# The softmax inverse of the middle stage moves from VectorE to GpSimd

## The reference

```
y = _cond_layer_norm(x, cond, ...)
scores = (q[src] . k[dst]);  ex = exp(scores - smax[src])
attn = ex / denom[src];      out = segment_sum(attn * v[dst]) @ wo + bo
x = x + out
y = relu(_cond_layer_norm(x, ...) @ m_w1 + m_b1) @ m_w2 + m_b2
x = x + y
```

## Time and profile before

| | |
|---|---|
| median of 3 runs | 1299.51 us (1297.67 to 1301.1) |
| the profiled execution | 1292.61 us, span 1290.8 us |
| mean granted TensorE clock | 0.955 |
| TensorE busy | 1171.9 us, 91% of the span |
| TensorE weight loads busy | 1058.0 us, 82% |
| VectorE busy | 831.9 us, 64% |
| GpSimd busy | 656.0 us, 51% |
| ScalarE busy | 487.3 us, 38% |
| the four bodies of the middle stage | about 290 to 815 us of the span |

### The profile page before, as it was taken

One profiled execution on the slowest core, in us unless ns is written; L12 is line 12 of the kernel. 1 busy time (PEld: TensorE's weight loads), 2 busy tenths in 40 slices (PEclk: granted clock), 3 DMA queues, 4 the chain that ended last, 5 costly groups with the idle time before them and its releaser, 6 DMA issues. The chain is left out here.

```text
span 1290.8 us, 21357 instructions
## 1 busy us (share of the span) xinstructions
PE 1171.9 (91%) x7134; PEld 1058.0 (82%) x7134; DVE 831.9 (64%) x1759; ACT 487.3 (38%) x873; POOL 656.0 (51%) x807
## 2 busy tenths in 40 slices
PE   7888779689999999999999999899999899999686
PEld 6778667569988998889988998778888688888674
DVE  7999787666766567566667576355556555565545
ACT  5334424124612353225521452344344343443311
POOL 3443562356557555766477555844116332235562
PEclk9889889689999999999999999999999989999788
DMA  5000001311212120230112113240010000011101
GB/s 112 1 1 1 22 10 59 117 47 40 74 42 74 52 75 1 75 91 10 66 42 74 43 65 121 73 122 1 1 66 34 1 33 1 1 66 33 65 33 40
DMA packets 40265, 60.81 MB, mean 47 GB/s; under 512 B 13864, under 2 KB 14114, under 8 KB 39537
## 3 DMA queue, kind: packets, MB, share of 16 engines
q1 hardware_dynamic: 40162, 59.47, 14.3%
HBM read 52.76 MB, written 5.41 MB: 45 GB/s over the span
## 5 line engine op out<-in xcount | busy, mean ns | idle before, releaser
L405 POOL TENSOR_SCALAR prob<-prob,rinv 125x628 f32<-125x628 f32 x160 | 126.2, 790 | 290.5 <-DVE rinv L399 289.1
L335 POOL TENSOR_TENSOR w_lo<-w_raw,w_hi 128x512 fp32r<-128x512 f32 x152 | 203.5, 1339 | 12.7
L295 PE MATMUL ps<-yt_hi,w_hi 128*128 128x314 f32 x640 | 203.1, 317 | 5.1 <-DVE yt_lo L1898 3.0
L295 PE MATMUL ps<-yt_hi,w_lo 128*128 128x314 f32 x640 | 198.5, 310 | 0.0
L295 PE MATMUL ps<-yt_lo,w_hi 128*128 128x314 f32 x640 | 198.2, 310 | 0.0
L633 PE MATMUL ps<-oh_s,oh_d 125*125 125x314 bf16 x800 | 124.4, 315 | 23.4 <-DVE oh_s L531 20.9
L633 PEld LDWEIGHTS ps<-oh_s,oh_d 125*125 125x125 bf16 x800 | 111.0, 145 | 36.6 <-DVE oh_s L531 30.3
L295 PEld LDWEIGHTS ps<-yt_hi,w_hi 128*128 128x128 f32 x640 | 122.6, 192 | 7.7 <-DVE yt_lo L1898 3.6
L358 ACT ACTIVATE pt_hi<-ps 125x625 fp32r<-125x625 f32 x160 | 108.1, 685 | 51.3 <-PE ps L317 50.6
L317 PE MATMUL ps<-ident,prob 125*125 125x125 f32 x800 | 117.7, 282 | 8.9 <-DVE pt_lo L1709 5.7
L332 POOL TENSOR_SCALAR w_hi<-w_raw 128x512 fp32r<-128x512 f32 x152 | 98.0, 645 | 53.9 <-DMA w_raw<-L_gnn_wo 37.4
(11 more groups left out here) (263 smaller groups left out, 2736.8 us busy)
## 6 DMA issues: line engine op xcount, KB each, us to landing
w_raw<-L_gnn_m_w SPq DMA_DIRECT2D x8, 1024.0 KB, 5.3
w_raw<-L_gnn_W SPq DMA_DIRECT2D x6, 1024.0 KB, 5.3
w_raw<-L_gnn_wv SPq DMA_DIRECT2D x4, 1024.0 KB, 5.6
w_raw<-L_gnn_wq SPq DMA_DIRECT2D x4, 1024.0 KB, 5.4
w_raw<-L_gnn_wk SPq DMA_DIRECT2D x4, 1024.0 KB, 7.2
w_raw<-L_gnn_wo SPq DMA_DIRECT2D x4, 1024.0 KB, 6.1
w_raw<-L_gnn_Wv SPq DMA_DIRECT2D x2, 1024.0 KB, 5.9
w_raw<-L_gnn_Wq SPq DMA_DIRECT2D x2, 1024.0 KB, 5.4
```

The lines of the kernel that those rows point to most:

```text
L295: ins = pe.matmul(out_ap, lhs(i, kk), rhs(j, kk), start=kk == 0 and n == 0, stop=kk == count - 1 and n == 2)
L335: pool.tensor_tensor(w[slot][1][:, kk, 0:cols], w_raw[slot][:, kk, 0:cols], w[slot][0][:, kk, 0:cols].bitcast(FP32), ALU.subtract).then_in ...
L405: pool.tensor_scalar(prob[:, u % RING_P, :], prob[:, u % RING_P, :], rinv[:, o:o + 1], 1.0, ALU.mult, ALU.mult).then_inc(scaled, 1)
```

## The change

The two inverse steps leave VectorE's table; the order of what is left in it and the tables of the other engines stay. On GpSimd every scaling in the middle stage is preceded by an addition of 1e-16 and a power of minus one (the exponent is a small tile set once at the start), each waiting for the one before it. GpSimd waits for ScalarE's exponential itself, and the semaphore `m_inverse` goes. The last stage keeps its inverse on VectorE.

```diff
 LOOP_DVE = """
-lo:k0 lo:q0 lo:k1 sc:s0_0 sc:s0_1 inv:s0_0 sc:s0_2 inv:s0_1 sc:s0_3 lo:q1 sc:s0_4 lo:t0_0 inv:s0_2 sc:s1_0
...
+lo:k0 lo:q0 lo:k1 sc:s0_0 sc:s0_1 sc:s0_2 sc:s0_3 lo:q1 sc:s0_4 lo:t0_0 sc:s1_0
...
-    def pool_scale(pool, u, it, units, rinv_done, scaled):
-        pool.wait_ge(rinv_done, it * units + u + 1)
+    def pool_inverse(pool, steps, o, before, ready):
+
+        pool.wait_ge(ready, before + 1)
+        own(pool)
+        steps.done(pool.tensor_scalar(rinv[:, o:o + 1], denom[:, o:o + 1], 1e-16, 1.0, ALU.add, ALU.mult))
+        steps.wait(pool)
+        steps.done(pool.tensor_tensor(rinv[:, o:o + 1], rinv[:, o:o + 1], neg_one[:, :], ALU.pow))
+
+    def pool_scale(pool, u, it, units, rinv_done, scaled, count=None):
+        pool.wait_ge(rinv_done, it * units + u + 1 if count is None else count)
         o = u % SMALL_RING
         own(pool)
         pool.tensor_scalar(prob[:, u % RING_P, :], prob[:, u % RING_P, :], rinv[:, o:o + 1], 1.0, ALU.mult,
...
+            steps.done(pool.memset(neg_one[:], -1.0))
...
-        loop = Steps(s_pm, 2 * TILES + 2 * 2 + 6 * C)
+        loop = Steps(s_pm, 2 * TILES + 2 * 2 + 6 * C + 2 * UNITS)
...
                 if kind == "scale":
-                    pool_scale(pool, int(name[1]) * TILES + int(name[3]), it, UNITS, s_ri, s_sc)
+                    u = int(name[1]) * TILES + int(name[3])
+                    pool_inverse(pool, steps, u % SMALL_RING, it * UNITS + u, s_ex)
+                    pool_scale(pool, u, it, UNITS, steps.sem, s_sc, steps.it * steps.per_body + steps.n)
...
-                elif kind == "inv":
-                    dve_inverse(dve, steps, int(name[1]) * TILES + t, it, UNITS, s_ex, s_ri)
```

More of the change, by code:

```diff
@@ L146 @@
 LOOP_DVE = """
-lo:k0 lo:q0 lo:k1 sc:s0_0 sc:s0_1 inv:s0_0 sc:s0_2 inv:s0_1 sc:s0_3 lo:q1 sc:s0_4 lo:t0_0 inv:s0_2 sc:s1_0
[L148 to L152, removed]
+lo:k0 lo:q0 lo:k1 sc:s0_0 sc:s0_1 sc:s0_2 sc:s0_3 lo:q1 sc:s0_4 lo:t0_0 sc:s1_0
+lo:t0_1 sc:s1_1 lo:t0_2 lo:q2 sc:s1_2 lo:t0_3 lo:t0_4 sc:s1_3 lo:k2
+lo:t1_0 sc:s1_4 sc:s2_0 lo:pv0 lo:t1_1 sc:s2_1 lo:q3 lo:t1_2 lo:k3 sc:s2_2 lo:t1_3 sc:s2_3 lo:t1_4 sc:s2_4 lo:t2_1 lo:t2_0 lo:pv1 sc:s3_0
+lo:t2_2 sc:s3_1 lo:t2_3 sc:s3_2 sc:s3_3 lo:t2_4 sc:s3_4 lo:t3_0 lo:t3_1 lo:t3_2 lo:t3_4 lo:t3_3 lo:pv2 lo:pv3 res:o0 st:o0 scl:n2_0 shift:n2_0 res:o1 st:o1 scl:n2_1 res:o2
 st:o2 lo:a2_0 shift:n2_1 res:o3 scl:n2_2 shift:n2_2 st:o3 lo:a2_1 scl:n2_3 shift:n2_3 lo:a2_2 res:o4 st:o4
@@ L240, in build @@
     neg_half = small("neg_half", [R, 1])
+    neg_one = small("neg_one", [R, 1])
     low = small("low", [R, SMALL_RING])
@@ L1146, in build @@
     s_hi, s_st, s_rs = sem("m_hi"), sem("m_stats"), sem("m_rstd")
-    s_ex, s_ri, s_sc = sem("m_exp"), sem("m_inverse"), sem("m_scaled")
+    s_ex, s_sc = sem("m_exp"), sem("m_scaled")
     s_vh, s_vd, s_xb = sem("m_v_hi"), sem("m_v_split"), sem("m_bias_added")
@@ L1377, in middle_dve @@
         v_lo(dve, 0, TILES - 1)
-        loop = Steps(s_vm, 2 * (2 * TILES) + UNITS)
+        loop = Steps(s_vm, 2 * (2 * TILES))
         last = Steps(s_vm2)
```

## The result

The changed kernel takes 1325.34 us (median of 4 runs, 1323.61 to 1327.59) against 1298.59 us before; the ratio is 1.0204, with a 95% interval from 1.0181 to 1.0227. The forecast was 1330, in a range from 1316 to 1342.

A forecast was written before the change was run, and what follows sets the result against it. TensorE was taken to bound the middle stage, with GpSimd's queue just in time. Three bodies of 4.7 + 3.3 = 8.0 us and a last of 6.8 made 30.8 us, added to a 1299.5 median: 1330 us, range 1316 to 1342.

The forecast's parts named there:

- What bounds the kernel: Middle stage: TensorE busy 498 of 505 us; vanished VectorE instructions can give back no more than TensorE's waits.
- reserve: Time between a scaling's end on GpSimd and its transposes' start, less about 0.2 us of way to TensorE.
- The cost of a unit: Addition and power ahead of each GpSimd scaling: 1.2 us in the loop (1.13 to 1.29), 1.1 in the last body.
- The twin outside the loop: `rstd`'s addition and power in the last body, written out with constants: a chain of 1.04 us.
- The head: Start of an attention: scalings s0_1 to s0_4 late, s1_0 not, TensorE 4.7 us late (4.2 in the last body).
- The tail: Last head of an attention: scalings one each 1.96 us, TensorE 3.3 us late (2.6 in the last body).
- rival 1: Only the head costs, the tail is swallowed by VectorE's freed queue: 17 us, 1316.5 us; chance 0.12.
- The last body: Fourth body, written out with constants: head 4.2 plus tail 2.6, 6.8 us.
- The waits: TensorE waits for GpSimd's `prob` some seven times a body, four at the head, three in the tail, about 32 us together.
- rival 2: TensorE's clock falls once in each body after its waits: 31 + 7 = 38 us, 1337 us; chance 0.10.
- Rival 3: No change: three tiles between a score and its transposes hide the longer chain, 1299.5 us; chance 0.04.
- Rival 4: Faster: VectorE, rid of 25 us, brings `pt_lo` forward and four waits of 0.6 us go, 1297 us; chance 0.04.

The follow-up runs named there:

- Run 6: Changed kernel with the middle stage's inverse left out on both engines, GpSimd scaling by the sum itself: 1296.96 us, ratio 0.999 to the kernel before.
- run 2: Kernel before, with only the eight middle units s1_1 to s2_3 of a body taking their inverse on GpSimd: 1297.96 us, ratio 0.9997.
- Run 3: Kernel before, with only s0_0 to s0_4 of a body taking their inverse on GpSimd: 1312.75 us, ratio 1.0099.
- Run 4: Kernel before, with only s2_4 and s3_0 to s3_4 of a body taking their inverse on GpSimd: 1307.02 us, ratio 1.0067.
- run 5: Changed kernel with a second power (exponent one) on GpSimd ahead of the first: 1364.09 us, ratio 1.0511 to the kernel before.
- run 1: The kernel before measured once more, no edit: 1298.69 us, ratio 0.9994.
- run 8: GpSimd order of Run 7, with s2_4 to s3_4 taking their inverse on VectorE again: 1295.84 us, ratio 0.9989 to the kernel before.
- 10: Kernel before, all inverses on VectorE, with GpSimd's order of Run 7: 1298.73 us, ratio 1.001.
- Run 7: Changed kernel with GpSimd's long work moved out from between the first and last heads' scalings: 1300.18 us, ratio 1.0016 to the kernel before.
- 9: The changed kernel measured once more, no edit: 1323.10 us, ratio 1.0195 to the kernel before.

## Why the prediction was right

**What bounds the kernel.** TensorE, with VectorE and GpSimd beside it. Run 6 shows the first half (an emptier VectorE shortens an attention by at most 0.03 us), run 2 the second (GpSimd may take 32 inverses where it has reserve).

**The cost of a unit.** I took 1.2 us in the loop and 1.1 in the last body, between 1.13 and 1.29. Measured is 1.03 us from the start of the addition to that of the scaling (451.85 to 452.88), and a pace of 1.91 us for a unit against the scaling's own 0.76, so 1.15 in a full queue. The twin outside the loop was the right one: the power follows the addition's start after 0.27 us, also in the loop, except behind `ws`. What I had added for register instructions isn't there between addition, power and scaling; the other 0.12 us of the 1.15 stand ahead of the addition, which starts 0.87 us behind the start of a scaling (466.46 and 467.33) where the next instruction used to start after 0.76. No run tells what they are. The last body is no cheaper in all this. The Trainium skill's ratio of about two for GpSimd (GPSIMD Engine Reference, "Engine selection"), weighed against the trace, was rightly not used for this size: the power takes 551 ns, 3.4 times the reciprocal's 164. Most of that is the power itself, since the addition, the same operation on both engines, takes 192 ns against 149.

**The head.** Forecast: waits at s0_1 to s0_4, none at s1_0, TensorE 4.7 us late; measured: these four and no other, 4.6 us. By the forecast's own working with measured terms, s0_4 is 5.23 us late and not 5.4 (the unit costs 1.15 us, not 1.2), its reserve is 0.74 and not 0.67 (the way from GpSimd to TensorE is 0.13 us, not 0.2), and from its transposes to those of s1_0 pass 5.42 us instead of 5.32, which the forecast did not have: 5.23 - 0.74 + 0.10 = 4.6. So the terms are off by a tenth or two and partly cancel. Run 3 shows the head alone.

**The tail.** Forecast 3.3 us, measured 2.9, with waits at s3_1, s3_3 and s3_4 as worked out; the 0.2 us that I had for s3_0 did not come. With the cheaper unit the working gives about 2.8. Run 4 shows the tail alone, so rival 1 falls.

**The last body.** Forecast 6.8 us, measured 7.15: this term was too small, since I had taken its unit to be cheaper than the loop's. The three loop bodies grew by 7.5 each, against 8.0.

**The waits.** Forecast about 32 us of waiting for `prob` in seven waits a body; the seven came, with 23.8 us. The rest of the cost stands as busy time: TensorE is busy for 254.9 us in the four attentions, and was for 247.5 before. 23.8 of waiting and 7.4 of busy time, less the 1.7 that the waits for `pt_lo` gave back, make 29.5. The last section says where the busy time comes from.

**The clock.** It stayed at 1.00 through waits of up to 1.6 us, so rival 2 falls for this kernel. The Trainium skill (TensorE: Matmul & The Clock Gate, "HAM oscillation — how this bites in real kernels") warns of gaps between bursts; rests of this size among matmuls did not bring the fall, and in run 5, with rests of up to 2.96 us, it came.

**The sum.** Forecast 30.8, the attentions have 29.6 and 29.2, the medians 27 and 25. So the mechanism and its terms are right within some 5%. Of the 5.0 us between 1330.3 and 1325.3, the terms make 1.2 (30.8 against 29.6), the median of before, 1299.5 then and 1298.6 now, makes 0.9, and 2.9 are left: the attentions grew by that much more than the time. The prediction had put everything outside the attentions at nothing, and there something seems to be given back. Median less attentions is 1298.7 - 249.9 = 1048.8 us for run 1 and 1325.3 - 279.5 = 1045.8 for the change; 1048.0, 1047.1, 1045.9 and 1048.8 for the other kernels with attentions of 62.5 us (runs 2, 6, 8, 10), 1045.3, 1047.6, 1046.0, 1044.7 and 1044.1 for those with longer ones (runs 3, 4, 5, 7, 9). The first five have a mean of 1047.7, the six with longer attentions of 1045.6: 2 us, though the two groups overlap (1045.9 to 1048.8 and 1044.1 to 1047.6). The traces place about half of it: from the end of the first attention to the start of the last, the other two attentions left out, the six traces with 62.5 us (the first of the kernel before among them) have 236.8 us on average and the others 235.6. One piece can be seen: where a body turns into the next, TensorE waits for "issue" in four traces of the six with 62.5 us (the kernel before twice, runs 2 and 8), and in none of the six with longer ones. The waits of the middle stage of run 1:

```profile
PE ps L295 <- issue: 1.1, 1, 1.1
```

Why this wait should go when TensorE is held up elsewhere no run tested, and a trace holds one execution. The cause of the 2 us stays open.

**No change, faster.** Rival 3 needed reserves that weren't there at head and tail. Run 7 makes them at the head and in part at the tail, and its interval just leaves out 1; run 8, which spares the tail, has an interval that holds 1. Rival 4 hoped for the waits for `pt_lo`; run 6 shows that they aren't VectorE's.

## What to carry to other kernels

An engine that idles for more than a third of a stage (GpSimd was busy 318 of 505 us) can still have no room where the work comes: before moving work to it, set the end of each of its results beside the start of the instruction that needs it, unit by unit, and add up only what exceeds these reserves. In a queue without gaps each added microsecond is passed on to all units behind it, and it ends only where the queue rests. If the moved work fits on average, the order of the other work on that engine is worth more than its speed: here the same instructions cost 27 us in one order and 2 in another (29.6 and 5.6 in the attentions).

## What the runs showed that was not expected

A wait of TensorE costs more than the idle time that the profile shows for it. In the second body's head the idle times are 1.56 + 0.44 + 1.27 + 0.32 = 3.59 us, and TensorE is 4.58 later: 0.25 us more for each wait. The records say where this stands. Matmuls in a stream start 0.14 or 0.15 us apart but are recorded as lasting 0.31, so at a wait some 0.16 us more of the last one count as busy; and the five transposes behind a wait last 0.80 instead of 0.71.

TensorE's clock fell in every body of run 5, where its waits for `prob` reach 2.96 us, and in no body of the change, where they reach 1.6; no run tells where between the two it begins. The fall cost nothing there, because GpSimd set the pace.

Small dependent instructions on GpSimd stand close: a power of a 125x1 tile starts 0.27 us behind the start of the addition it waits for, and a second power 0.62 behind the first, which itself takes 0.55. Ahead of a scaling of 628 columns that reads the result 0.21 us of idle stand each time, in the loop and outside.
